# A two-batch attention pipeline whose main loop is written out in a line on four engines

## What is computed

```python
x = L0(x, ctx)      # 16 heads: causal self-attention, attention to ctx, FFN, three layer norms
x = L1(ctx, x)      # one head, a gate of width 4, self-attention of the result, skips
x = L2(x, ctx)      # softmax(x ctx^T) ctx + x
# L3: 8 heads against ctx, then a recurrence over the 128 tokens
U = (layernorm(x) @ W_in.T + b_in) @ Bmat
def step(s, u_t):
    s = silu(s @ A.T) + u_t
    return s, s
x = x + states @ Cmat + (program_probs.mean(1) @ W_prog.T + b_prog)
```

## Time and profile before

| | us |
|---|---|
| median of 3 runs | 4619.35 (4616.46 to 4643.11) |
| the profiled execution | 4596.14 |
| its span | 4594.3 |
| granted TensorE clock, mean | 0.977 |

### The profile page before, as it was taken

How to read it: one execution, slowest core, us unless ns; L and a number is a source line. 1 busy time by engine, 2 the same in 40 slices (tenths; PEclk the granted TensorE clock), 3 DMA queues, 4 the chain that set the end, 5 groups by cost and what they waited for, 6 DMA issues and landing times.

```text
span 4594.3 us, 127885 instructions
## 1 busy us (share of the span) xinstructions
PE 4326.0 (94%) x38309; PEld 3617.0 (79%) x38309; DVE 3785.2 (82%) x10020; ACT 2755.3 (60%) x5761; POOL 2121.7 (46%) x2084
## 2 busy tenths in 40 slices
PE   1899999999999999999999999999999999999859
PEld 1678888888888888888888888888888888888745
DVE  2688888888888888888888888888888888888734
ACT  0466666666666666666666666666666666666522
POOL 0244444445544544444455445544544454455425
PEclk9899999999999999999999999999999999999979
DMA  3001000000000000000000000010000000000036
GB/s 96 17 20 30 19 27 27 29 17 29 27 29 17 27 29 20 26 27 29 17 29 27 29 17 29 27 29 17 27 29 19 28 27 29 17 29 25 19 83 262
DMA packets 127391, 156.21 MB, mean 34 GB/s; under 512 B 23925, under 2 KB 114362, under 8 KB 122618
## 3 DMA queue, kind: packets, MB, share of 16 engines
q1 hardware_dynamic: 127034, 152.93, 10.8%
HBM read 115.01 MB, written 37.88 MB: 33 GB/s over the span
## 4 chain that ended last, share of the span: by engine, by line
PE 82%; issue 6%; DVE 6%; POOL 1%; DMA 1%; DVEq 1%; ACT 1%; SPq 0%; ACTq 0%; POOLq 0%
PE bank L611 17%; PE bank L619 12%; PE bank L681 12%; PE bank L603 8%; PE bank L651 7%; PE bank L711 4%; PE bank L792 4%; PE bank L724 4%; PE bank L706 3%; PE bank L841 2%; PE bank L630 2%; DVE mx L1072 2%; DVE prob L1083 1%; PE bank L1459 1%; PE bank L1467 1%
## 5 line engine op out<-in xcount | busy, mean ns | idle before, releaser
L928 ACT ACTIVATE prob<-prob 128x512 f32<-128x512 f32 x1280 | 781.7, 635 | 656.7 <-DVE prob L1083 655.8
L1072 DVE TENSOR_REDUCE mx<-bank 128x4 f32<-128x512 f32 x1280 | 843.1, 680 | 74.8 <-PE bank L651 66.3
L1336 POOL TENSOR_TENSOR rs_ln<-ve_ln,half 128x2 f32<-128x2 f32 x320 | 226.0, 706 | 1428.8 <-DVE ve_ln L1051 1428.7
L1083 DVE TENSOR_TENSOR prob<-bank,mx 128x512 f32<-128x512 f32 x1280 | 850.0, 681 | 26.1 <-PE bank L681 7.6
L918 ACT ACTIVATE turned<-bank 128x512 f32<-128x512 f32 x960 | 546.5, 597 | 522.4 <-PE bank L603 400.9
L938 ACT ACTIVATE probT<-bank 128x512 f32<-128x512 f32 x1280 | 722.7, 601 | 175.7 <-PE bank L681 161.4
L681 PE MATMUL bank<-ident,prob 128*128 128x128 f32 x5120 | 760.9, 287 | 13.1 <-ACT prob L928 8.7
L681 PEld LDWEIGHTS bank<-ident,prob 128*128 128x128 f32 x5120 | 609.2, 148 | 108.1 <-issue 46.3
L611 PE MATMUL bank<-turned,shared 128*128 128x256 f32 x2560 | 614.7, 383 | 2.0 <-ACT turned L918 1.9
L611 PEld LDWEIGHTS bank<-turned,shared 128*128 128x128 f32 x2560 | 467.8, 191 | 78.3 <-issue 22.9
L1383 POOL TENSOR_SCALAR shared<-turned,half_of 128x512 f32<-128x512 f32 x256 | 399.4, 1570 | 138.6 <-ACT turned L918 138.6
(11 more groups left out here) (215 smaller groups left out, 8291.0 us busy)
## 6 DMA issues: line engine op xcount, KB each, us to landing
shared<-in_x SPq DMA_DIRECT2D x128, 256.0 KB, 3.8
CB<-in_ctx SPq DMA_DIRECT2D x64, 256.0 KB, 3.5
CC<-in_ctx SPq DMA_DIRECT2D x64, 256.0 KB, 2.7
mod<-mod_rows SPq DMA_DIRECT2D x64, 256.0 KB, 3.4
residual<-X SPq DMA_DIRECT2D x64, 256.0 KB, 3.6
out<-turned SPq DMA_DIRECT2D x16, 1024.0 KB, 4.8
turned<-residual SPq DMA_DIRECT2D x14, 1024.0 KB, 6.8
shared<-in_ctxb SPq DMA_DIRECT2D x2, 2048.0 KB, 7.4
```

What stands on the lines that cost most here:

```text
L928: nc.scalar.activation(flat(t), flat(t), ACT.Exp, scale=SCALE[p]).then_inc(*st["act"].mark(f"exp.{b}{r}"))
L1072: nc.vector.tensor_reduce(m[:], banks.of(f"{att}.tile.{b}{r}")[:, :].rearrange("p (h t) -> p h t", h=4), AX, ALU.max)\
L1083: nc.vector.tensor_tensor(t[:], banks.of(f"{att}.tile.{b}{r}")[:, :].rearrange("p (h t) -> p h t", h=4), maxes.of(f"{att}.max.{b}{r}")[:]. ...
```

## The change

`drive` no longer makes a loop for engines whose entry in `IN_ROW` is NG: their 70 iterations all stand in a line, and with a plain number for the group every wait is on a constant. SP has no entry and keeps the loop as it was. Order of steps, banks, buffers and lags are the same.

```diff
+IN_ROW = {"pe": NG, "act": NG, "dve": NG, "pool": NG}
+
+
 def drive(eng, rings, handlers, engine, meanwhile=None):
...
-    for i in range(LAGS + 1):
+    row = IN_ROW.get(engine, 1)
+    first = NG if row >= NG else LAGS + 1
+    if first < NG:
+        assert (NG - first) % row == 0
+    for i in range(first):
         body(i, i, False)
-    if NG > LAGS + 1:
-        with eng.Fori(LAGS + 1, NG) as i:
-            body(i, LAGS + 1, True)
-    for i in range(max(NG, LAGS + 1), NG + LAGS):
+    n = first
+    if first < NG:
+        with eng.Fori(first, NG, row) as i:
+            for k in range(row):
+                body(i + k if k else i, first + k, True)
+        n += row
+    for i in range(NG, NG + LAGS):
         if meanwhile is not None and i == NG + LAGS - 2:
             meanwhile()
-        body(i, LAGS + 2 + i - NG, False)
+        body(i, n + i - NG, False)
```

## The result

The changed kernel takes 4469.24 us (median of 4 runs, 4467.88 to 4469.49). The kernel before, run beside it on the same chip, takes 4627.85 us (4616.46 to 4643.11). The ratio is 0.9655, with a 95% interval from 0.9621 to 0.9688, so 3.4% are gained. The forecast was 4501 us with a range from 4470 to 4540.

The account below looks back on a forecast made before the run. PE was taken as the bound, held up by DVE's back edge: 114 us for edges plus 23 for the clock less 17 for code blocks gave a 118 us gain, 4619 - 118 = 4501 us, range 4470 to 4540.

Parts of the forecast that it names:

- The bound and the wait: PE, busy 94% of the span, bounds the kernel; DVE's back edge makes it wait at `len`, 74.1 us in 54 times.
- 56 x 2.03 us for the edges: Loop's back edges: removing 56 gains 114 us, all through DVE's edge; PE's shows no wait, ACT's and POOL's cost nothing.
- 0.41 us an iteration for the clock: Loop iterations: average loss to granted-clock falls after PE's idleness at `len`; 23 us in all to be regained.
- the rival that the falls hang on something else in the iteration: Loop: clock falls stay at their old rate, perhaps from the load burst; 4525 us, chance 0.12.
- 58 iterations at 64.23 take 3725.3: Every iteration takes as long as 63 to 64 did in the kernel before; gain 118.1 us against the profile.
- marks 6 to 64: A mark is an iteration's first `mix_out.u` matmul on PE; 6 to 64 took 3843.4 us before, 3725.3 forecast.
- Less 57 x 0.3 = 17 for the blocks: PE in a line reads four to five code blocks an iteration, priced at 0.3 us: 64.23 against 63.92.
- I carry that over: The median's 23 us (0.5%) above the profiled execution was kept for the changed kernel: 4619 - 118 = 4501 us.
- Code reading: Rival: PE's reading of in-line code becomes the bound; 4791 us if none hidden, 4646 if half exposed; slower, chance 0.05.
- stall at block ends: Rival: DVE or ACT stalls 2 us once an iteration at the worst place, giving the gap back; 4600 us.
- The gap did come with the branch: Rival denied this: DVE's gap before `nz_self` stays; gain below 20, about 4600 us; gap or its like stays, 0.09.
- The rule of 108 ns: Skill's compare-and-branch time, cited against the forecast: 56 edges worth 6 us; the trace shows 2.17 us idleness at one.

Follow-up runs that it names:

- dve_line: Against the kernel before, only DVE's iterations stand in a line, all other engines keep their loops: 4490.30 us, ratio 0.9730.
- dve_loop: The changed kernel with DVE alone keeping its loop, PE, ACT and POOL in a line: 4648.01 us, ratio 1.0080 to the kernel before.
- turned_list: The kernel before, all loops kept, with the first 40 steps of DVE's list moved to its end: 4522.24 us, ratio 0.9796.
- dve_pe_line: Only DVE and PE in a line, ACT and POOL keep their loops: 4449.24 us, ratio 0.9682 to the kernel before.
- pause: The changed kernel with three unused reductions on DVE ahead of `nz` in iterations 8 to 63: 4566.02 us, ratio 0.9896 to the kernel before.
- pause4: The changed kernel with four unused reductions on DVE ahead of `nz`: 4638.38 us, ratio 1.0091 to the kernel before.
- pe_three: The changed kernel with PE looping again, over three groups at a time (18 back edges): 4633.08 us, ratio 1.0084 to the kernel before.
- act_loop: The changed kernel with ACT alone keeping its loop: 4449.34 us, ratio 0.9669 to the kernel before.
- dve_pe_again: Second run of the kernel with only DVE and PE in a line, ACT and POOL looping: 4449.50 us, ratio 0.9672 to the kernel before.
- dve_half: The changed kernel with DVE looping over iterations 7 to 34 and in a line from 35 on: 4560.46 us, ratio 0.9931 to the kernel before.
- after_again: The changed kernel itself, run once more on another occasion: 4466.42 us, ratio 0.9709 to the kernel before.

## Why the prediction was right and where it was wrong

**The bound and the wait.** Right. PE bounds the kernel, DVE's back edge stood in front of `len`, and without it the wait is gone rather than smaller. dve_line and dve_loop show that the edge is DVE's, and turned_list that it costs by its place. The time of an iteration came inside the forecast's 63.9 to 64.4 us.

**56 x 2.03 us for the edges.** Nearly right in sum. I ascribed it to DVE's edge alone, but PE's own loop, which I had called free, has a share: between dve_line (64.47 an iteration) and dve_pe_line (63.79) lie 0.7 us, of which the 14 falls explain 0.35 (an iteration with one takes 65.5 us in dve_line, without one 64.1). Among iterations without a fall, 65.94 before, 64.14 in dve_line and 63.78 in dve_pe_line, 1.80 us belong to DVE's edge and 0.36 to PE's loop, 2.16 together where I had 2.03. In the change itself most of PE's share went to ACT, below.

**0.41 us an iteration for the clock.** Right in kind and size: 23 us over 25 falls are 0.9 us for each. In dve_line a fall costs 1.4 us, perhaps because PE has no wait there that absorbs it. One fall was left after the change. `pause` and `pause4` speak against the rival that the falls hang on something else in the iteration, and against the load burst speak pe_three, with 18 falls outside it, and dve_pe_line, with the burst and none. Open are the falls without idleness: 14 in dve_line and 7 in turned_list, where PE keeps its loop, and the one left in the changed kernel, where it doesn't.

**The sum.** "58 iterations at 64.23 take 3725.3" was a little high: marks 6 to 64 lie at 372.82 and 4093.33, 3720.5 us, so 64.15 each. That is 4.8 us less, and what stands behind mark 64 was 3.9 us shorter (374.4 against 378.3 to the end of the span). Profile against profile 126.7 us are gained where I had 118.1.

**"Less 57 x 0.3 = 17 for the blocks".** Right in size, wrong in cause. I had measured 64.23 against 63.92 between iterations that differ in every engine's program, and put the difference down to PE's reading of code. act_loop reads the same code of PE at 63.78. The 0.31 us by which the changed kernel is longer are ACT's program in a line. That my difference had the same size is partly luck: in dve_pe_again the step from mark 6 to mark 7 takes 64.11 us where the later ones take 63.77, so a single such step was a poor measure. Had I known, the better kernel would have stood in the prediction.

**"I carry that over".** This is the step that failed. The median before lay 23 us above the profiled execution, and I added these 23 us to the time after. But the excess belongs to the kernel before and didn't come along: the changed kernel's median, 4469.24, stands 0.3 us below its own profiled execution, 4469.49. On the two occasions where both ran, the kernel before took 4627.85 and 4596.14 us and the changed one 4469.24 and 4466.42: 32 us apart and 3. Within these occasions the changed kernel's runs lie within 1.6 and 3.6 us, those before within 27 and 31. So the 4478 us of the profile stood for the median too, and 4478 less 8.6, by which the gain between the profiles was larger than forecast, is the 4469 measured.

Why the kernel before has this excess is shown in part. The profiled 4596.14 is not one of the runs behind its median, so some of the 23 us may lie between chips; on the three later occasions the same kernel took 4593.69 to 4613.72. On the last occasion its time goes with its mean clock (4586.62 us at 0.979, 4596 at 0.977, 4617 at 0.970, so about 3 us for each 0.001), and in dve_half and dve_loop likewise (4615.58 at 0.973, 4670.49 at 0.953). But on the occasion of dve_line its 13 runs lie within 10 us at clocks from 0.967 to 0.974 in no such order, and for the four runs at 4627.85 no clock is known. It isn't PE's idleness alone either, since the runs of `pause` and `pause4` hardly differ.

From median to median 158.6 us are gained, of which 126.7 is seen between the profiles and nearly all of the other 31.9 is the excess of the runs before over their profiled one (4627.85 - 4596.14 = 31.7).

**The rivals.** Code reading never became the bound: queue 8 brought 317 packets, in the band of 300 to 350, and PE's list of waits has 0.2 us of "issue". No stall at block ends showed on DVE. The gap did come with the branch. The rule of 108 ns for a compare-and-branch (the Trainium skill, "Advanced Engine Details and Errata", Control Flow Timing) would give 6 us, where DVE's loop costs over 100 (dve_line, 0.027 of 4614 us, with the falls): the rule lacks the read of code that the trace shows at each edge.

## What to carry to other kernels

A loop's back edge costs by what stands right behind it and by whether its target must be read again: turn the body so that nothing urgent follows the edge, or write the loop out, and only on the engines whose edge reaches the bound. Look for packets of the instruction queues in the gap: they tell a read of code from other "issue". If the runs of a kernel differ by more than those of its relatives, ask what makes them differ before adding the excess to a forecast for a kernel without it. Price a difference between two iterations only after asking in how many engines they differ.

## What the hardware showed that I had not expected

- Idleness of 0.86 to 1.5 us once in 66 us is enough for the granted clock to fall to 0.50 in 17 to 38 of 56 iterations, for 3.4 or 6.8 us each time (pause, before, pause4, dve_loop); PE's own loop, with no wait in the list, brings 14 in dve_line.
- A back edge to code that is read again stands PE for 6.4 us on average in two pieces (pe_three), and the period with it is 8.9 us longer. Each piece ends 1.2 to 1.8 us after a packet of queue 8 has landed.
- DVE's edge reads code each time though its body has only 374 instructions: a packet of queue 14 at each of 56 edges, and 1.6 to 1.8 us from its landing to the next step (before).
- With a delay made of work in place of the branch, 35 falls of the clock and all, the runs of a kernel lie within 0.06% (pause4); those of the kernel before on the same chip within 0.3%, and those of dve_loop within 1.2%.
- Writing out ACT's program slows PE by 0.31 us in each 64 us with PE never idle (after_again against act_loop). Why stays open.
